# The second attention of a two-layer transformer: both batches' head quads in one sequence

## The reference

```python
x = layernorm(x + L0_attn(x))   # 16 heads, fourth power in place of softmax
x = layernorm(x + L0_ffn(x))    # 2 experts, the better one for each token
x = layernorm(x + L1_attn(x))   # below
x = layernorm(x + L1_ffn(x))    # 32 experts, 6 for each token, and a shared one

def L1_attn(x):                 # B, T, C = 2, 1024, 256; H = 32, dh = 8
    q, k, v = [split_heads(x @ W.T + b) for W, b in ((Wq, bq), (Wk, bk), (Wv, bv))]
    q, k = [apply_rope(apply_rope(t, freqs_abs), freqs_temp) for t in (q, k)]
    scores = einsum('bhqd,bhkd->bhqk', q, k) / sqrt(dh)
    scores = where(causal, scores, -inf)
    weights = softmax(scores)
    return einsum('bhqk,bhkd->bhqd', weights, v).reshape(B, T, C) @ Wo.T + bo
```

## Time and profile before

| | us |
|---|---|
| median of 3 runs | 1758.84 |
| lowest and highest | 1757.13, 1761.33 |
| the profiled execution | 1752.08 |
| its span, first to last instruction | 1750.3 |
| PE busy | 1389.3 (79%) |
| DVE busy | 1089.2 (62%) |
| ACT busy | 830.9 (47%) |
| POOL busy | 569.0 (33%) |

### The profile page before, as it was taken

One profiled execution on the slowest core, in us unless ns is written; L12 is line 12 of the kernel. 1 busy time (PEld: TensorE's weight loads), 2 busy tenths in 40 slices (PEclk: granted clock), 3 DMA queues, 4 the chain that ended last, 5 costly groups with the idle time before them and its releaser, 6 DMA issues.

```text
span 1750.3 us, 25040 instructions
## 1 busy us (share of the span) xinstructions
PE 1389.3 (79%) x9104; PEld 879.1 (50%) x9104; DVE 1089.2 (62%) x2297; ACT 830.9 (47%) x1221; POOL 569.0 (33%) x666
## 2 busy tenths in 40 slices
PE   5477837675799996688888886789788887999992
PEld 4233523342578775344444354444334335699981
DVE  7678786866443545667666525575777626455676
ACT  2476436654433331246665631355456552166660
POOL 7477254655110111101001000010037302776661
PEclk8589966987889998579999997588789996999996
DMA  2690000002201100000000000000002134477775
GB/s 83 235 336 1 1 0 1 1 15 91 81 28 46 40 19 25 0 1 1 1 1 1 1 1 1 1 1 1 1 31 92 60 146 184 159 217 208 247 264 215
DMA packets 69069, 124.23 MB, mean 71 GB/s; under 512 B 7318, under 2 KB 55126, under 8 KB 67928
## 3 DMA queue, kind: packets, MB, share of 16 engines
q1 hardware_dynamic: 56664, 85.92, 15.2%
q0 software_dynamic: 12288, 36.72, 5.7%
HBM read 60.22 MB, written 62.39 MB: 70 GB/s over the span
## 4 chain that ended last, share of the span: by engine, by line
PE 57%; DVE 25%; ACT 8%; POOL 5%; issue 3%; DMA 1%; POOLq 0%; SPq 0%; DVEq 0%; ACTq 0%
PE psum L1902 10%; PE psum L1776 8%; DVE neg_max L2438 6%; PE psum L2085 5%; DVE probs L2456 5%; PE psum L1875 5%; PE psum L1836 5%; PE psum L1992 4%; ACT probs L2198 4%; PE psum L2108 3%; PE psum L2013 3%; PE psum L1887 3%; PE psum L318 2%; POOL probs L2977 2%; PE psum L1852 2%
## 5 line engine op out<-in xcount | busy, mean ns | idle before, releaser
L2198 ACT ACTIVATE probs<-psum 128x1024 f32<-128x1024 f32 (+1 forms) x480 | 435.5, 945 | 317.9 <-PE psum L1887 157.8
L2438 DVE TENSOR_REDUCE neg_max<-psum 128x1 f32<-128x512 f32 (+3 forms) x768 | 382.4, 551 | 204.5 <-PE psum L1852 180.9
L1902 PE MATMUL psum<-probs,v 128*32 128x512 f32 (+3 forms) x2304 | 263.0, 560 | 55.8 <-POOL probs L2977 42.3
L1836 PE MATMUL psum<-kt,qt 32*128 32x512 f32 (+3 forms) x768 | 225.3, 474 | 69.7 <-DVE neg_max L2438 67.5
L1875 PE MATMUL psum<-qt,kt 32*128 32x512 f32 (+6 forms) x1152 | 247.2, 463 | 41.5 <-ACT probs L2198 23.0
L2456 DVE TENSOR_TENSOR probs<-probs 128x1024 f32<-128x1024 f32 (+1 forms) x152 | 200.3, 1375 | 43.6 <-ACT probs L2198 43.2
L1875 PEld LDWEIGHTS psum<-qt,kt 32*128 32x128 f32 (+1 forms) x1152 | 111.5, 203 | 221.1 <-issue 84.6
L323 POOL TENSOR_SCALAR q_rows<-neg_max 128x16 fp32r<-128x16 f32 x32 | 7.0, 219 | 602.2 <-DVE neg_max L2446 340.4
L1836 PEld LDWEIGHTS psum<-kt,qt 32*128 32x128 f32 x768 | 100.2, 205 | 118.2 <-DVE neg_max L2438 111.2
L3046 POOL DMA_INDIRECT results<-sp_y,sp_row x128 | 124.6, 974 | 58.5 <-ACT sp_y L2253 29.8
L1776 PE MATMUL psum<-ident,q_rows 128*128 128x128 f32 x384 | 69.5, 326 | 76.4 <-ACT k_rows L2127 53.0
(11 more groups left out here) (315 smaller groups left out, 2514.6 us busy)
## 6 DMA issues: line engine op xcount, KB each, us to landing
many_x<-blank SPq DMA_DIRECT2D x2, 10240.0 KB, 49.6
sp_xs<-many_x SPq DMA_DIRECT2D x64, 320.0 KB, 3.6
sp_w<-in_sparse SPq DMA_DIRECT2D x8, 1280.0 KB, 11.4
x_turned<-results SPq DMA_DIRECT2D x8, 768.0 KB, 6.5
sp_back<-results SPq DMA_DIRECT2D x8, 768.0 KB, 9.1
sorted_x<-blank SPq DMA_DIRECT2D x2, 1152.0 KB, 7.7
sorted_y<-y SPq DMA_DIRECT2D x18, 128.0 KB, 1.7
rows<-in_x SPq DMA_DIRECT2D x4, 512.0 KB, 7.0
```

The lines of the kernel that those rows point to most:

```text
L1836: scored_max[0] = pe.matmul(psum[:, base:base + (k1 - k0) * P], A.qt[rows, q_slot, tile * P:(tile + 1) * P], A.kt[rows, k_slot, k0 * P:k1 ...
L1902: inst = pe.matmul(psum[32 * h:32 * h + 32, bank + q0:bank + QCH], A.v[:, key, col:col + 32], A.probs[:, slot, h, at:at + QCH - q0], start ...
L2198: act.activation(dst, view, ACT.Exp if A.softmax else ACT.Square).then_inc(exped.by(A.layer, b, quad, c, step, h0), 1)
L2438: inst = dve.tensor_reduce(A.neg_max[:, g % 2, 0 if last else 1, tile, h0 + i:h0 + i + 1], bank[:, at * P:(at + cols) * P], X_AXIS, ALU.ma ...
```

## The change

The second attention gets a planner of its own, `plan_second_attention`. It lays the quads of both batches as one sequence, G from 0 to 15.

- The second batch is transposed (`bring_x`) and projected beside quads 5 and 6 (G == 5 and G == 6), its first quad is cut beside quad 6 and turned at that quad's end, and the maxima of quad 8 stand beside quad 7. So quads 8 and 9 are laid like all others.
- The second batch's v can't overwrite the first one's, which is still read. It goes to `late_v`, which lies in `stage`, and is filled with ones by a POOL instruction in the setup, once `stage` is free.
- The products of the rotation went to `probs`, which is in use then. They go to the fourth slot of `kt`, so the ring of `kt` has three slots in place of four.
- The second half of the first batch's output projection, with its layer norms, stands beside quads 8 and 9.
- Place 7 of the turn is now 7.2, so in all quads it is issued ahead of the second half of step 7, and no longer ahead of its first.
- The number of projections, transposes, scores, maxima and exponents is as before.

```diff
     def rotated(self, u, which):
+        if u is None:
+            return self.kt_plain[:, 3, which * QCH:(which + 1) * QCH]
         return self.probs[:, u // 2, 2 * (u % 2) + which, :]
+
+    def v_of(self, b):
+        return self.late_v if self.softmax and b else self.v
...
+        attention1.late_v = stage[:, 0:TILES * attention1.v_row].rearrange("p (t r) -> p t r", t=TILES)
...
+            def plan_second_attention(A, start, late, during, tail, amid):
...
+                q_ring, probs_ring, oc_ring, kt_ring = Ring(2), Ring(WEIGHTS_AHEAD + 3), Ring(2), Ring(3)
...
+                def project(b, t):
+                    slot, slot_free = pairs.take()
+                    u = (b, 0 if b else t % ROTATING)
...
+                    do("project", A=A, b=b, t=t, slot=slot, slot_free=slot_free, xt_done=xt_done[b, t // 4], w_ready=w_ready,
+                       before=(*start, *qk_free[b]), u_free=u_free.get(u, ()))
...
+                    qk_free[1] = (*done[0], *done[1]) if b == 0 else qk_free[1]
...
+                last = BATCH * quads - 1
+                for G in range(last + 1):
+                    b, quad = divmod(G, quads)
...
+                    if 0 < G < last:
+                        for n, plan in enumerate(PLAN_OF_STEP):
+                            if plan is not None:
+                                for half in range(2):
+                                    beside[2 * n + half].append((G + 1, plan, 2 - 2 * half))
+                        between += [(2.8, lambda: cut_max(G + 1, 0)), (5, lambda: turn_max(G + 1, 0))]
+                    if G + 2 <= last:
+                        at = {quads - 3: 2.6, quads - 2: 4.2}.get(G, 3.5)
+                        between += [(at, lambda: cut(G + 2)), (7.2, lambda: turn(G + 2))]
+                    if quad:
+                        between.append((2.5, lambda: normalize(G - 1)))
+                    elif b:
+                        between += [(1, lambda: normalize_half(0, 1)), (2.2, lambda: turn_out(0, 1)), (3.4, lambda: project_out(0, 1)),
+                                    (6, norm)]
+                    if (b, quad) == (1, 1):
+                        between.append((4, norm))
+                    if G == quads - 3:
+                        between += [(1.2, lambda: bring_x(1, 0)), (3.2, lambda: bring_x(1, 1))]
+                        between += [(5.4 + 0.9 * t, lambda t=t: project(1, t)) for t in range(5)]
+                    if G == quads - 2:
+                        between += [(0.6 + 1.1 * (t - 5), lambda t=t: project(1, t)) for t in range(5, TILES)]
+                    if quad == quads - 1:
+                        between += [(5.5, lambda: normalize_half(b, 0)), (7, lambda: turn_out(b, 0)), (8.5, lambda: project_out(b, 0))]
...
-            free, unwound, norms = plan_attention(attention1, free, late, during=during_second, tail=tail, amid=amid_last)
+            free, unwound, norms = plan_second_attention(attention1, free, late, during_second, tail, amid_last)
...
-                        inst = pe.matmul(psum[32 * h:32 * h + 32, bank + q0:bank + QCH], A.v[:, key, col:col + 32],
+                        inst = pe.matmul(psum[32 * h:32 * h + 32, bank + q0:bank + QCH], A.v_of(b)[:, key, col:col + 32],
...
-                u = t % ROTATING
+                u = None if A.softmax and b else t % ROTATING
...
+                if A.softmax:
+                    q.wait_ge(pool_cut, "wo", L)
+                    q.wait_ge(dve_cut, "w", L)
+                    pool.memset(A.late_v, 1.0).then_inc(pool_set.by("late v", L), 1)
```

More of the change, by code:

```diff
@@ L1816, in turn, with max_unit @@
                            ).then_inc(turned.by("k", A.layer, b, g, t0), 1)
-            def max_unit(A, b, maxima, **_):
+            def max_unit(A, maxima, **_):
                 score_maxima(A, maxima, range(2))
-                mask_maxima(A, b, maxima)
+                mask_maxima(A, maxima)
             def score_maxima(A, maxima, which):
-                g, plan, h0, banks, free, q_slot, k_slot, rows_ready = maxima.values()
+                b, g, plan, h0, banks, free, q_slot, k_slot, rows_ready = maxima.values()
                 parts, masked = MAX_PLANS[plan]
@@ L1839, in score_maxima, with mask_maxima @@
                                 skip_group_check=True)
-            def mask_maxima(A, b, maxima):
-                g, plan, h0, banks = [maxima[name] for name in ("g", "plan", "h0", "banks")]
+            def mask_maxima(A, maxima):
+                b, g, plan, h0, banks = [maxima[name] for name in ("b", "g", "plan", "h0", "banks")]
                 masked = MAX_PLANS[plan][1]
@@ L2146, in project @@
                 q.wait_ge(projected, A.layer, b, t)
-                q.wait_ge(pool_set, "v", A.layer)
+                q.wait_ge(pool_set, "late v" if A.softmax and b else "v", A.layer)
                 for e in before:
                     q.wait_ge(*e)
-                vv = A.v[:, t, 0:H * (A.d + 1)].rearrange("p (h e) -> p h e", h=H)[:, :, 0:A.d]
+                vv = A.v_of(b)[:, t, 0:H * (A.d + 1)].rearrange("p (h e) -> p h e", h=H)[:, :, 0:A.d]
                 copy(vv, psum[:, base + 512:base + 768].rearrange("p (h e) -> p h e", h=H)
@@ L2425, in cut, with max_unit @@
                                ).then_inc(dve_cut.by(*name, 2), 1)
-            def max_unit(A, b, before, maxima):
-                g, plan, h0, banks = [maxima[name] for name in ("g", "plan", "h0", "banks")]
+            def max_unit(A, before, maxima):
+                b, g, plan, h0, banks = [maxima[name] for name in ("b", "g", "plan", "h0", "banks")]
                 parts = MAX_PLANS[plan][0]
@@ L2450, in scores @@
                 if maxima:
-                    max_unit(A, b, before, maxima)
+                    max_unit(A, before, maxima)
                 if A.softmax or on_pool:
```

250 lines of the change are left out of this document (added).

## The result

| | before | after |
|---|---|---|
| median of the runs (us) | 1760.09 (4 runs, 1757.13 to 1762.02) | 1744.62 (4 runs, 1742.31 to 1746.38) |
| ratio to before, 95% interval | | 0.9913 [0.9892, 0.9934] |
| span of the profiled execution (us) | 1750.3 | 1740.6 |
| forecast | | 1713, range 1696 to 1731 |

The kernel is faster by 15.5 us, a third of the 46 us forecast, and the time lies outside the range.

What follows compares the result with a forecast made beforehand. PE was taken to bound ordinary quads (30.3 of 34.6 us). Five quads 173.0, clock dips 5.3 and added work made 233.0 against 279.0, 46.0 less: 1758.8 - 46.0 = 1712.8, or 1713 us, range 1696 to 1731.

Steps and rivals of the forecast that it cites:

- The gap goes: Between quads 7 and 8: the 61.7 us without exponents vanish; the stretch falls from 279.0 to 233.0 us.
- the prediction's own signs of being wrong: Quad 5 under 51 or over 63 us; quads with only the turn moved changing by more than 0.3 us; others.
- The inserted work: Quads 5 to 9: projections 27.2, bring_x 4.4, output projection 14.2, half normalizations 1.9, layer norms 7.0 us.
- The norm in quad 9: Layer norm beside quad 9, one of two priced at 3.5 us each, between 0 and 6.6.
- The clock dips a little even in ordinary quads ... so I add 5.3: Quads 5 to 9: 5.3 us for clock dips, from quads 1 to 6 taking 212.9 against 207.6.
- all-or-nothing rival of 1826: Stretch of quads 5 to 9: waits behind projections drop PE's clock to 1.2 GHz, +113 us; chance 0.04.
- The turn at 7.2 for 7 ... I take 0, since the bank pair is as free there as before: Turn's new place in twelve quads: priced at 0 us, between -0.1 and +1.0 each.
- The high end written there, +1.0: Turn at 7.2: +1.0 us each if copies to qt and kt hold up the second half of step 7.
- The rival: Turn's new place costs a copy in each quad, 12 x 1.0 us, quads 1 to 4 at 35.6: 1725; chance 0.05.
- twelve turns: The prediction's count of quads whose turn moves from 7 to 7.2.
- Late_v's fill, the cut of quad 7, three slots of kt: Setup and quads' ordering: taken as covered and given no price; the fill uncovered would cost its 2.2 us once.
- DVE late at times: Quad 5: DVE not the bound, only late at times; rival with it late behind every projection, 1729, chance 0.13.

Runs made afterwards that it cites:

- e1: Changed kernel with the turn set back from 7.2 to 7 in all quads; ratio to the kernel before 0.9818.
- e4: Changed kernel with VectorE's rotation of the second batch left out, so its q and k are not computed; ratio to the kernel before 0.9805.
- e6: Changed kernel with the turn at 7 and quad 5's projections at places 5, 6, 7, 8, 9; 1722.00 us, ratio to the kernel before 0.9792.
- e7: e6 with the second batch's rotation on GpSimd, after ScalarE copies q and k to SBUF; 1716.73 us, ratio to the kernel before 0.9758.
- e9: Changed kernel with its own places (turn at 7.2, projections 5.4 to 9.0) and only the rotation moved to GpSimd; ratio to the kernel before 0.9708.
- e3: Changed kernel with quad 5's projections at whole places 5 to 9, turn left at 7.2; ratio to the kernel before 0.9876.
- e2: Kernel before with only the turn moved from 7 to 7.2; ratio to the kernel before 1.0119, 21.5 us slower.
- e8: e7 with the rotation on VectorE, from SBUF after ScalarE's copy, instead of GpSimd; ratio to the kernel before 0.9850.
- e5: Changed kernel run again without any edit; 1746.72 us, ratio to the kernel before 0.9918.

## Why the prediction was wrong

- *The gap goes*: right. The stretch is rebuilt as forecast, no wait holds the second batch's projection, and 60 us without exponents are gone. Two of the prediction's own signs of being wrong came in: quad 5 at 66.7, over 63, and quad 4, which only has the turn moved, longer by 1.0, over 0.3.
- *The inserted work*: about right, or sized a little too dear. As an estimate, take the clock out at 0.43 us for each us at the low level (e1, e4) and 1.0 for the turn (quad 4). Quad 5 keeps 66.7 - 9.2 - 35.6 = 21.9 for five projections and two `bring_x`, forecast 21.4. Quad 6 keeps 48.2 - 4.1 - 35.6 = 8.5 for three, forecast 10.2. Quads 7, 8 and 9 keep 6.1, 6.9 and 1.9. Together 45.3, against 54.7 in the forecast (27.2 + 4.4 + 14.2 + 1.9 + 7.0). The 1.0 for the turn is shown in quad 4 and not here; see below. The norm in quad 9 leaves the wait of 3.50 at 1161.17 that the earlier trace rows has, but the quad as a whole keeps only 1.9 for it.
- *"The clock dips a little even in ordinary quads ... so I add 5.3"*: this term failed in its size. It took the clock of quads without inserted work for that of quads with it. The stretch is at the low level for 51.2 us, at 0.34 to 0.43 some 17 to 22 us. A second reading is near that: PE is busy for 208.0 us with work that the prediction added up to 189 at full clock. The clock fell in quad 5 behind waits of 1.9 and 1.5 us. The runs that took away waits for the rotation brought quad 5 to 0.94 (e4, e6, e7, e9), but for e3, which stayed at 0.84. Against the first trace, part of what they won in quad 5 was lost again in quads 7 and 8. Over quads 5 to 9 the low level lasts 40 to 49 us in e3, e4, e6, e7 and e9, and 51 and 66 in the changed kernel's two traces. So most of this loss stays whatever the rotation does, and what sets it is not shown. The forecast named this danger as an all-or-nothing rival of 1826; it came as a fraction, 12 to 17 us over the term.
- *"The turn at 7.2 for 7 ... I take 0, since the bank pair is as free there as before"*: this step failed too. The high end written there, +1.0, is what it costs, and quads 1 to 4 were to take 35.6: quad 4 does. The prediction looked at the pair of banks that the turn takes. What it overlooked are the single banks of the maxima: the turn's 2.15 us gave DVE the time to free one, and without it PE waits 0.35 and runs one maximum alone for 0.43. The pair costs little (0.06 with its wait of 0.24). The price is not the same everywhere. It is 1.0 in quad 4 at full clock (e1, e2), 0.9 in quad 6 (e7, e9) and less than nothing in quad 7 (e8). With the low stretches that move with it, it is 11.1 in quads 0 to 4 of the two traces of this case, 7.8 in the mean of all, and 6.7 in quads 10 to 15, with e6 and e7 back at 238.0 and 237.8 in the latter. In quads 5 to 9 it is 0.7 (e3, e6) and, with the places, 1.6 (e9, e7); e1 takes 247.9 there, between the changed kernel's two traces. The rival had a chance of 0.05, a price of 12 and quad 4 at 35.6, but gave ACT's copies as the cause. The prediction also counts twelve turns, where quads 0 to 13 all have one.
- *The sum of the errors*: quads 5 to 9 took 12.3 us over the forecast (245.3 against 233.0). With 0.43 and 1.0 for each turn this is clock +16.7, turn +5.0 and inserted work -9.4; with 0.34 and a turn worth 1 in the whole stretch it is about +12, +1 and -1. The sum is measured, the split is an estimate. With 11.1 and 6.7 outside the stretch, where the prediction had no change, that is 30.1 us. The attention's later start (5.3) and the stages behind it (0.9) bring it, but for rounding, to the 36.2 by which the profiled execution lies over the 1706.1 of the prediction. The median lies 31.8 over 1712.8.
- *Late_v's fill, the cut of quad 7, three slots of kt*: priced at nothing, and no wait on them is found. The projections in quad 5 were to be "DVE late at times": true, 4.5 + 0.9 us of bank and 6.0 of reductions over two quads.

Settled only in size: how much of the gain of the rotation on GpSimd is waits and how much is clock. Of the 15.4 us by which e9 is under the mean of the changed kernel's two traces in quads 5 to 9, PE's busy time for the same matmuls gives 8.9 (203.1 against 208.0 and 216.0), by the clock and by matmuls that no longer run alone, and its waits the other 6.5. Which wait taken away moved the clock is open. The rate of 0.43 is the upper of what quad 7 gives: against the changed kernel's 41.7 at full clock, e4 (43.2, 3.5 us low) gives 0.43 and e5 (44.1, 7.1 us low) 0.34; against e8's 42.3, e7 (45.3, 7.2 us low) gives 0.42. At 0.34 the clock term would be 17 us and the inserted work 50.

## What to carry to other kernels

When work is put between the steps of a loop that is bound by PE, look first at what stands behind it in the queue of the engine that reads its result: moving eight rotations from VectorE to the idle GpSimd was worth 15.4 us against the mean of the changed kernel's two traces in quads 5 to 9 (248.9 against 233.5), and freeing their banks alone was worth less than nothing. When a unit is moved, ask what it gave the other engines time for where it stood. A place moved by a fraction of a step can count once for every turn of the loop, and it must be priced like an edit of its own; run both signs of it, in the old kernel and in the new. Price the clock from a stretch that has the same kind of waits, not from the smooth stretch next to it.

## What the runs showed of the hardware

- Single waits of 1.5 to 1.9 us on PE, in a stretch otherwise full of matmuls, were followed by a granted clock of 1.2 GHz (windows from 957.1 and 967.3), and PE worked through all of these low stretches.
- Two executions of the changed kernel differed by 7 us in quads 5 to 9 (245.3 and 252.4), with 51 and 66 us at the low level in them, while the medians agreed to 2 us (1744.6 and 1746.7).
- A rotation of one tile took GpSimd 3.8 us in four instructions (0.61, 0.62, 1.28, 1.28) and VectorE 2.1 by the earlier trace rows; the slower engine gave the faster kernel.
- In a half step of full-clock scores, two score matmuls and two for the maxima started within 0.01 us and were through after 0.44. Where the last of them had to wait for its bank, it ran 0.43 by itself behind the wait of 0.35 (quad 4, before and after).
